# A two-layer graph network on one core: the middle group's one-hot product covers 168 of a unit's 256 edge slots

## What is computed

```python
edge_index = jnp.stack([src, dst])
h = jnp.maximum(_layernorm(x, axis=-1), 0.0)
x = x + _L0_gnn_ref(h, relation_embedding, W1, b1, w2, edge_index, edge_type_200)
h = jnp.maximum(_layernorm(x, axis=-1), 0.0)
x = x + _L1_gnn_ref(h, src, dst)
...
def _L0_gnn_ref(x, ...):
    triple = jnp.concatenate([x[src], x[dst], relation_embedding[edge_type]], axis=1)
    c = triple @ W1 + b1
    b = jax.nn.leaky_relu(c @ w2, SLOPE)
    alpha = softmax of b over the edges of one dst
    out = jax.ops.segment_sum(c * alpha[:, None], dst, num_segments=n)
    return jax.nn.leaky_relu(out, SLOPE)
...
def _L1_gnn_ref(feats, src, dst):
    agg = jax.ops.segment_sum(feats[src], dst, num_segments=n_nodes)
    return jnp.where((deg > 0)[:, None], agg, feats)
```

## Time and profile before

| | |
|---|---|
| timed runs, median of 3 | 1653.2 us (1652.97 to 1653.62) |
| span of the profiled execution | 1763.7 us |
| PE busy | 1519.0 us (86%) |
| DVE busy | 1494.8 us (85%) |
| ACT busy | 1348.3 us (76%) |
| POOL busy | 1117.9 us (63%) |

### The profile page before, as it was taken

The page is one execution under the profiler, slowest core; times in us unless marked ns, Lnnn a source line. Parts: engine busy times, 40 slices in busy tenths (PEclk is TensorE's granted clock), DMA queues, the critical chain, the costliest instruction groups (busy, mean ns, idle before and its releaser), DMA issues.

```text
span 1763.7 us, 34877 instructions
## 1 busy us (share of the span) xinstructions
PE 1519.0 (86%) x12139; PEld 1361.0 (77%) x12139; DVE 1494.8 (85%) x4210; ACT 1348.3 (76%) x3528; POOL 1117.9 (63%) x994
## 2 busy tenths in 40 slices
PE   1379999999999999999999983688888888888887
PEld 0269999999999999999989982466666666666665
DVE  5549999999999999999989886587887887888877
ACT  0268988888988888888878962677777777777776
POOL 5756767776667676767766104666666666666660
PEclk9889999999999999999999996789899999899899
DMA  4634666666666666666656455477777777777753
GB/s 106 169 102 111 176 179 171 178 174 185 172 167 178 169 165 187 173 176 166 177 151 173 124 165 141 103 202 196 197 203 199 194 202 202 192 201 205 189 149 106
DMA packets 469367, 298.80 MB, mean 169 GB/s; under 512 B 35662, under 2 KB 438084, under 8 KB 469190
## 3 DMA queue, kind: packets, MB, share of 16 engines
q1 hardware_dynamic: 433942, 243.28, 49.8%
q0 software_dynamic: 35248, 53.28, 12.6%
HBM read 203.78 MB, written 104.34 MB: 175 GB/s over the span
## 4 chain that ended last, share of the span: by engine, by line
PE 45%; ACT 30%; another core or an unknown queue 8%; DVE 6%; issue 5%; POOL 1%; DMA 0%; SPq 0%; DVEq 0%; POOLq 0%
ACT cs L1542 16%; ACT cs L1547 8%; PE c_p L1616 6%; PE t_p L1602 6%; PE c_p L1617 5%; PE c_p L1619 4%; PE t_p L1599 3%; PE t_p L1604 3%; PE t_p L1603 3%; PE y_p L1632 3%; PE y_p L1634 3%; PE y_p L1635 3%; PE y_p L1633 3%; ACT an L1525 2%
## 5 line engine op out<-in xcount | busy, mean ns | idle before, releaser
L1111 POOL DMA_INDIRECT xe<-in_x,idx_t x516 | 635.7, 1232 | 290.4 <-ACT ae L1528 164.2
L1120 POOL DMA_INDIRECT xe<-x_d,idx x332 | 335.6, 1011 | 184.7 <-issue 90.5
L1542 ACT ACTIVATE cs<-xn,nbias,rstd 128x128 f32<-128x128 f32 x782 | 311.0, 480 | 91.7 <-remote 91.7
L1525 ACT ACTIVATE an<-xn,nbias,rstd 128x128 f32<-128x128 f32 x783 | 326.6, 482 | 3.1 <-DVE nbias L1255 3.1
L1221 DVE BATCH_NORM_STATS2 st<-xn 128x6 f32<-128x256 f32 x843 | 309.7, 413 | 2.2 <-DMA xe<-in_x,idx_t 1.7
L1528 ACT ACTIVATE ae<-xe,nbias,rstd 128x128 f32<-128x128 f32 x522 | 226.2, 482 | 0.0
L1616 PE MATMUL c_p<-w1a,th 128*128 128x129 f32 x1044 | 217.4, 290 | 8.2 <-issue 8.2
L1617 PE MATMUL c_p<-w1b,th 128*128 128x129 f32 x1044 | 203.8, 277 | 3.1 <-issue 3.0
L1560 ACT ACTIVATE cs<-c_p 128x258 f32<-128x258 f32 x261 | 100.5, 385 | 129.2 <-PE c_p L1621 76.4
L1331 DVE TENSOR_SCALAR sel<-row,plc_t,alpha 128x256 f32<-128x256 bf16 x522 | 192.9, 410 | 3.4
L1221 DVE BATCH_NORM_STATS2 st<-xe 128x6 f32<-128x256 f32 x446 | 174.0, 410 | 17.9 <-DMA xe<-x_d,idx 17.9
(11 more groups left out here) (207 smaller groups left out, 3729.7 us busy)
## 6 DMA issues: line engine op xcount, KB each, us to landing
xn<-in_x SPq DMA_DIRECT2D x130, 384.0 KB
x_d<-xn SPq DMA_DIRECT2D x130, 384.0 KB
xn<-x_d SPq DMA_DIRECT2D x194, 256.0 KB
out<-xn SPq DMA_DIRECT2D x194, 256.0 KB
plr<-place_d SPq DMA_DIRECT2D x65, 256.0 KB
tyr<-types_d SPq DMA_DIRECT2D x65, 256.0 KB
xe<-in_x,idx_t POOLq DMA_INDIRECT x522
xe<-x_d,idx POOLq DMA_INDIRECT x332
```

Source lines behind the costliest of these rows:

```text
L1111: nc.gpsimd.indirect_dma_start(out=xe_of(u)[:, e, :], out_offset=None, in_=x, in_offset=bass.IndirectOffsetOnAxis(ap=idx_t[:, j:j + 1], ax ...
L1120: nc.gpsimd.indirect_dma_start(out=xe2_of(u)[:, k, :], out_offset=None, in_=x1_d, in_offset=bass.IndirectOffsetOnAxis(ap=idx2[:, j:j + 1], ...
L1525: a(an[:, u % 2, i, :], xs_of(u)[:, i, :], ACT.Relu, bias=nbias[:, j % 2, c:c + 1], scale=rstd[:, j % 2, c:c + 1])
L1542: a(own2_[:, u % 3, g, :], xs2_of(u)[:, g, :], ACT.Relu, bias=nbias[:, j % 2, c:c + 1], scale=rstd[:, j % 2, c:c + 1])
```

## The change

Two things change. In `turn` the three one-hot products stand in another order, and the product of the middle group covers slots 24 to 191 in place of 0 to 255. The two outer products, which don't overlap, come first and clear their half each; the middle one is added onto them. In the check, two conditions are added that make sure of it: slot 23 of tile 0 must still belong to group 0, and slot 64 of tile 1 (192 of the unit) to group 2 or to none.

```diff
+MID0, MID1 = 24, 192
...
-        over = part(2 * TC)[0:TU].rearrange("p (j k) -> p j k", k=TC)
+        over = part(4 * TC)[0:TU].rearrange("p (j k) -> p j k", k=TC)
...
                 v.tensor_scalar(over[:, 0, :], pl[:, :, 1, 0], 0.0, None, ALU.is_lt)
+                v.tensor_scalar(over[:, 2, :], pl[:, :, 0, MID0 - 1], float(P), None, ALU.is_ge)
+                v.tensor_scalar(over[:, 3, :], pl[:, :, 1, MID1 - P], float(2 * P), None, ALU.is_lt)
                 steps.then(v.tensor_scalar(over[:, 1, :], pl[:, :, 1, P], float(SLOTS), None, ALU.is_lt))
...
-                    mm(to[:, SLOTS:2 * SLOTS], an[:, u % 2, 1, :], one[:, P:3 * P], start=True, stop=False, skip_group_check=True)
-                    mm(to[:, SLOTS:SLOTS + P], an[:, u % 2, 0, :], one[:, 0:P], start=False, stop=True, skip_group_check=True)
-                    mm(to[:, SLOTS + P:2 * SLOTS], an[:, u % 2, 2, :], one[:, 3 * P:4 * P], start=False, stop=True, skip_group_check=True
-                       ).then_inc(s_turn, 1)
+                    mm(to[:, SLOTS:SLOTS + P], an[:, u % 2, 0, :], one[:, 0:P], start=True, stop=False, skip_group_check=True)
+                    mm(to[:, SLOTS + P:2 * SLOTS], an[:, u % 2, 2, :], one[:, 3 * P:4 * P], start=True, stop=False, skip_group_check=True)
+                    mm(to[:, SLOTS + MID0:SLOTS + MID1], an[:, u % 2, 1, :], one[:, P + MID0:P + MID1], start=False, stop=True,
+                       skip_group_check=True).then_inc(s_turn, 1)
```

## The result

The changed kernel takes 34,488 us (median of 4 runs, 34,473 to 34,502) against 1653.4 us: a ratio of 20.85, interval 20.83 to 20.88. Nothing in the first layer was slower, since the first layer did not run. The page of the changed kernel says so in its first line and in its lines of cost.

The account below looks back on a forecast made before the run. The prediction took PE as the bound, DVE just behind it and the bound after the cut. Terms of -16.5, -5, -3 and +0.1 us sum to -24.4, so 1653.2 becomes 1628.8, say 1629 us; range 1617 to 1642.

Parts of the forecast that it names:

- rival 4: Tables' check: it fires and the slow general path runs, many times as long; chance 0.01, shared with anything else slower.
- The cut: Middle product in the first layer, 256 to 168 columns: saves 0.145 us a unit on PE, bounds 0.14 and 0.15.
- The order and the flag: The three products in the first layer: their new order and start=True clearing two halves cost nothing.
- PE the bound before, DVE after: First layer, 200 to 900 us: PE is the bound, and after the cut DVE, with 674.1 us of work, takes over.
- One sign missed: Sign expected in the changed profile, 200 to 900 us: PE's busy share down to 96 to 98%.
- rival 3: First layer: PE idles more, its clock falls, each fall costing 3.4 us, and the kernel gets slower; chance 0.02.
- The check's cost: Tables' check: two more operations on 87x3 cost 0.1 us, bounds 0 and 0.3.
- The term of 3 us for 100 to 200 us: First units: 29 x 0.145 = 4.2 us, of which 3 are taken because PE is kept waiting for part.
- The terms of the two ends: First layer: gains of 3 us from 100 to 200 us and 5 us from 900 to 1,043 us.
- the middle term: First layer, 200 to 900 us: 683.5 us with 2.5 us of DVE's waits kept, a gain of 16.5 us.
- rival 1's half-way case: First layer: DVE's records are partly elastic, giving 1616 to 1621 us; chance 0.14 together with PE staying the bound, 1615.
- rival 2: First layer: PE and DVE lock together, stopping each other, 1640 to 1650 us; chance 0.16.

Follow-up runs that it names:

- e2: Kernel before, with its 256-column product, plus only the condition on slot 192 with limit 256: 34,570 us (one run).
- e1: Changed kernel with the limit of the slot 192 condition corrected from 256 to 128: 1635.9 us against 1654.4, ratio 0.989.
- e3: Changed kernel without the condition on slot 192, the one on slot 23 kept: 1640.4 us, ratio 0.991.
- f1: Changed kernel with the slot 192 limit corrected to 128 and start=True on the first outer product only: 1636.6 us against 1652.8, ratio 0.990.
- f4: Kernel before, uncut, with the slope left out on half of the first layer's features: 1642.9 us, ratio 0.994.
- f3: As f1, with the slope left out on half of the first layer's features: 1610.2 us, ratio 0.974.
- e4: Kernel before with the three products in the new order, the middle one still 256 columns wide, no condition added: 1653.5 us, ratio 0.9997.
- f2: As f1, with the middle product cut further to slots 40 to 167, 128 columns: 1632.9 us, ratio 0.987.

## Why the prediction was wrong

**The step that failed** is the dismissal of rival 4, "The check fires and the slow general path runs". I gave it 0.01 on the reading that "the two conditions ask that slot 23 be in group 0 and slot 192 not in groups 0 or 1". That is what the conditions are for; the second asks something else. I counted the edges of groups 0 and 1 over dst (165 at the most, fewer than 192) and compared the count with the intention, not with the expression. The count that would have decided it evaluates the line as written, with the base of tile 1, and gives 155 units of 261. The section on the change repeats the intention ("to group 2 or to none") in the place of what the line tests. e2 shows that this comparison alone makes the time 34,570 us, and e1 and e3 that nothing else in the change does. The chance of 0.01 for this rival was not bad luck: on these inputs it fires every time.

**The rest of the working** can be judged by f1, since the change minus its slip does what the prediction priced.
- *The cut, 0.145 us a unit.* Right: 0.44 to 0.29 us in the timelines, and 0.139 a unit between f4 and f3. The 0.13 ns a column that the prediction worked out from the Trainium skill ("TensorE: Matmul & The Clock Gate", Back-to-back issue gap) would have given 0.046; the traces disagree with it.
- *The order and the flag, nothing.* Right in time: e4 0.9997, f1 as e1.
- *PE the bound before, DVE after.* Right from 200 to 900 us: DVE 98.8% busy, PE's waits at L1605 for selT, f2's nearly useless cut, f3's 26 us. The period was forecast at 683.5/191.5 = 3.569 us and is 3.553. One sign missed: PE's busy share is 98.4%, where 96 to 98 was forecast.
- *The clock.* It stayed at 1.00 from 200 to 900 us though PE idled more; rival 3 did not come.
- *The check's cost, 0.1 us.* 0.13.
- *The size.* The forecast was -24.4 us; f1 gives -16.2, e1 -18.5, e3 -14.1. Between 200 and 900 us it is 193 x (3.627 - 3.553) = 14.3 us for the 16.5 of the sum, and that nearness is in part luck, as told below. The term of 3 us for 100 to 200 us is nothing: 116 records of the product pass there with the cut and without. I had seen DVE busy 80.3 of 100 us; the first row below, of e4, has it at 95.2, so it has no room. From 900 us on PE is the bound in f1 too, as forecast (second row, of f1: PE 59.8 of 60 us, DVE 56.2), but 25.5 to 29 units are left there and not 38, so 0.145 us on each is 4 and not 5, an estimate.

```profile
100.00:200.00 100.00, 98.89 (x946) 95.70 (x945) 95.23 (x264) 90.88 (x237) 79.89 (x67) 1.00 0.57 155
```

```profile
900.00:960.00 60.00, 59.79 (x595) 58.58 (x595) 56.24 (x156) 55.25 (x144) 20.53 (x16) 1.00 0.49 134
```

The three corrected terms give 18 us. The traces themselves have 16.6 at the end of the messages: the last record of the first message product starts at 1003.5 us in e4 and at 986.9 in f1.

The terms of the two ends were too big because they were read from a profiled execution that was 110.5 us longer than the timed ones: at 100 us it had 3 units behind it, where e4 has 10, so its DVE still had room and it had more units left at 900. I had noted the gap and carried the difference in us over unchanged. Most of the gap lies where the change does not reach, in the second layer. Its L1542 on ACT, before and then in e4 (duration in ns, then first and last start in us):

```profile
L1542 ACT ACTIVATE cs<-xn,nbias,rstd x782: 477/479/497, 1090.6 to 1750.8; 128x128 f32<-128x128 f32 x196
L1542 ACT ACTIVATE cs<-xn,nbias,rstd x782: 477/479/489, 1051.9 to 1636.0; 128x128 f32<-128x128 f32 x196
```

That is 660 us against 584, 76 of the 115 us between the two profiles, with the same code and the same 479 ns an instruction. Before, the profile puts 91.7 us of idle time ahead of this line, released by something that it calls "remote", and in e4 none; what it was stays open.

For the middle term the slow profile is one half of the account. The same working on e4's rows gives 700 - 9.6 + 2.5 = 692.9 us, a gain of 7 us, half of the measured 14.3. The sum holds DVE's work in a unit fixed, and it was not quite: 683.33/193 = 3.541 us in e4, 691.80/197 = 3.512 in f1, or 5.6 us over 193 units. That points the way of rival 1's half-way case; nothing was run to test it. So the 16.5 came near by two errors that partly cancel: the profile that it was read from showed more DVE idle time than e4's (25.9 us against 16.7), and DVE's work in a unit was taken as rigid. What share rival 2, the engines stopping each other, has in the missing 8 us was not separated.

## What to carry to other kernels

A condition that guards a fast path is part of the change's cost: evaluate it as it is written, on the data and with the base of every index in it, before pricing anything behind it. One wrong limit was worth 32,800 us here and the cut 16. And when the engine behind the bound is within 3% of it, a cut on the bound is worth about the distance between the two (in e4 PE is busy 3.608 us a unit and DVE 3.541, 0.067 apart, and the cut gave 0.074); f1 against e4 and f3 against f4 are the same cut without and with room on DVE, and the room doubled its worth. A profile whose span is far from the timed median should be taken as a picture of the order of waits, not of the idle time that can be won.

## What the runs showed of the hardware

Two profiled executions of nearly the same program differ by 115 us, 76 of them in the second layer: 1763.7 us before, 1648.9 for e4, whose timed medians are 1653.4 and 1653.5. A granted clock of 1.00 was kept from 200 to 900 us with PE idle 19 us of 700 (f2); in the earlier trace rows PE was idle 1.4 of 5 us, and over the 10 us behind that the granted clock was 0.66. An f32 product's time in the stream is in proportion to its columns: 0.44 us for 256, 0.29 for 168 and 0.22 for 128, so 1.72 to 1.73 ns a column at each width and no fixed part that can be seen. Three products with two start flags among them and with one take the same time (e1 0.989, f1 0.990 of before).
